# Graph network on one core: node scores spread over the partitions with two full-precision matmuls instead of four reduced-precision ones

## What is computed

```python
y = x @ w
s = y @ a
A = s[..., :, None] + s[..., None, :]
A = jnp.tanh(A / 8.0) * 8.0
A = jnp.where(A >= 0, A, 0.1 * A)
A = jnp.exp(A) * A_shape
A = A / jnp.sum(A, axis=-1, keepdims=True)
A = A * jnp.sum(A_shape, axis=-1, keepdims=True)
out = A @ x @ w
```

## Time and profile before

| | us |
|---|---|
| median of 3 runs | 1437.08 (1436.98 to 1437.58) |
| the profiled execution | 1435.79 |
| its span, first to last instruction | 1433.8 |
| PE busy | 1392.3 (97%) |
| DVE busy | 1287.9 (90%) |
| ACT busy | 990.5 (69%) |
| POOL busy | 947.7 (66%) |

### The profile page before, as it was taken

One profiled execution on the slowest core, in us unless ns is written; L12 is line 12 of the kernel. 1 busy time (PEld: TensorE's weight loads), 2 busy tenths in 40 slices (PEclk: granted clock), 3 DMA queues, 4 the chain that ended last, 5 costly groups with the idle time before them and its releaser, 6 DMA issues.

```text
span 1433.8 us, 34585 instructions
## 1 busy us (share of the span) xinstructions
PE 1392.3 (97%) x10900; PEld 1331.7 (93%) x10900; DVE 1287.9 (90%) x4001; ACT 990.5 (69%) x2312; POOL 947.7 (66%) x1876
## 2 busy tenths in 40 slices
PE   3799999999999999999999999999999999999997
PEld 2799999999999999999999999999999999999996
DVE  5789999999999999999999999999999999999984
ACT  3577777777777777777777777777777777777763
POOL 2676676676676676676676676676676676676652
PEclk9999999999999999999999999999999999999999
DMA  7011110120110110110110110110110110110100
GB/s 187 1 42 27 52 51 26 51 51 26 51 51 26 51 51 26 51 51 26 51 51 26 51 51 26 51 51 26 51 51 26 51 51 26 51 51 26 37 19 23
DMA packets 83078, 62.70 MB, mean 44 GB/s; under 512 B 40304, under 2 KB 65520, under 8 KB 83056
## 3 DMA queue, kind: packets, MB, share of 16 engines
q1 hardware_dynamic: 83056, 62.43, 15.8%
HBM read 45.62 MB, written 16.78 MB: 44 GB/s over the span
## 4 chain that ended last, share of the span: by engine, by line
PE 95%; DVE 2%; ACT 1%; issue 0%; DMA 0%; POOL 0%; SPq 0%; DVEq 0%; POOLq 0%
PE BANK L365 29%; PE BANK L330 24%; PE BANK L372 15%; PE WIDE L365 8%; PE WIDE L341 8%; PE WIDE L372 4%; PE BANK L357 2%; PE BANK L315 2%; PE BANK L384 2%; DMA TMP_D<-in_l2wt 0%; PE WIDE L278 0%; DVE BN_B L550 0%; DVE BN_C L550 0%; ACT UHI_D L444 0%; PE WIDE L284 0%
## 5 line engine op out<-in xcount | busy, mean ns | idle before, releaser
L444 ACT ACTIVATE UHI_B<-BANK 128x512 fp32r<-128x512 f32 x96 | 57.0, 593 | 43.9 <-PE BANK L330 43.9
L444 ACT ACTIVATE UHI_D<-BANK 128x512 fp32r<-128x512 f32 x96 | 57.1, 595 | 41.1 <-PE BANK L330 41.1
L444 ACT ACTIVATE UHI_C<-BANK 128x512 fp32r<-128x512 f32 x96 | 57.0, 594 | 41.0 <-PE BANK L330 41.0
L444 ACT ACTIVATE UHI_A<-BANK 128x512 fp32r<-128x512 f32 x96 | 57.1, 594 | 39.1 <-PE BANK L330 39.1
L599 DVE TENSOR_TENSOR ULO_D<-BANK,UHI_D 128x512 fp32r<-128x512 f32 x96 | 65.2, 680 | 18.7 <-ACT UHI_D L444 18.0
L732 POOL TENSOR_TENSOR LN_A<-MV_A,EPS 128x2 f32<-128x2 f32 x80 | 15.9, 198 | 92.3 <-DVE MV_A L558 92.3
L599 DVE TENSOR_TENSOR ULO_A<-BANK,UHI_A 128x512 fp32r<-128x512 f32 x96 | 65.2, 680 | 12.3 <-ACT UHI_A L444 11.8
L599 DVE TENSOR_TENSOR ULO_C<-BANK,UHI_C 128x512 fp32r<-128x512 f32 x96 | 65.1, 678 | 11.1 <-ACT UHI_C L444 9.3
L599 DVE TENSOR_TENSOR ULO_B<-BANK,UHI_B 128x512 fp32r<-128x512 f32 x96 | 65.7, 684 | 10.4 <-ACT UHI_B L444 8.5
L732 POOL TENSOR_TENSOR LN_D<-MV_D,EPS 128x2 f32<-128x2 f32 x80 | 15.8, 197 | 84.7 <-DVE MV_D L558 84.7
L732 POOL TENSOR_TENSOR LN_B<-MV_B,EPS 128x2 f32<-128x2 f32 x80 | 16.7, 209 | 78.2 <-DVE MV_B L558 78.2
(11 more groups left out here) (500 smaller groups left out, 6009.6 us busy)
## 6 DMA issues: line engine op xcount, KB each, us to landing
X_A<-in_xs SPq DMA_DIRECT2D x16, 256.0 KB, 2.8
X_B<-in_xs SPq DMA_DIRECT2D x16, 256.0 KB, 2.8
X_C<-in_xs SPq DMA_DIRECT2D x16, 256.0 KB, 2.8
X_D<-in_xs SPq DMA_DIRECT2D x16, 256.0 KB, 2.8
out_rows<-O_A SPq DMA_DIRECT2D x16, 256.0 KB, 2.0
out_rows<-O_B SPq DMA_DIRECT2D x16, 256.0 KB, 2.1
out_rows<-O_C SPq DMA_DIRECT2D x16, 256.0 KB, 2.1
out_rows<-O_D SPq DMA_DIRECT2D x16, 256.0 KB, 2.1
```

The source lines that it names most:

```text
L444: nc.scalar.activation(UHI[s][:, 0:J * D], bank(s, step)[:, :], ACT.Copy).then_inc(sem(f"c{step}"), 1)
```

## The change

The scores are no longer split. Steps 2H and 2L go from VectorE's list, and with them the tiles SHI and SLO and the reduced copy of the identity. TensorE's 3S waits for s_ready instead of scores_split, and does one matmul for each graph, on fp32 operands, instead of two on fp32r operands. All other steps keep their slots, and so their order.

```diff
-    "2U": 47.94, "2W": 50.48, "2S": 51.69, "2A": 52.99, "2N": 56.85, "2H": 56.91, "2L": 59.70, "3L": 66.92,
+    "2U": 47.94, "2W": 50.48, "2S": 51.69, "2A": 52.99, "2N": 56.85, "3L": 66.92,
...
-        IDENTR = sb("IDENTR", [P, P], F32R)
...
-        SHI = per_stream("SHI", J, dt=F32R)
-        SLO = per_stream("SLO", J, dt=F32R)
...
             def spread_scores(s, c, k):
 
-                pe.wait_ge(sem("scores_split"), c["n1"])
+                pe.wait_ge(sem("s_ready"), c["n1"])
                 bank_free(s, "3S", k)
                 for j in range(J):
-                    for part in (SHI, SLO):
-                        last = nc.tensor.matmul(bank(s, "3S")[:, j * P:(j + 1) * P], part[s][:, j:j + 1].to_broadcast([P, P]),
-                                                IDENTR[:, :], start=(part is SHI), stop=(part is SLO))
+                    last = nc.tensor.matmul(bank(s, "3S")[:, j * P:(j + 1) * P], ST[s][:, SC, j:j + 1].to_broadcast([P, P]),
+                                            IDENT[:, :], start=True, stop=True)
                 last.then_inc(sem("p3S"), 1)
...
                 dve.wait_ge(sem("ident_ready"), 1)
-                nc.vector.tensor_copy(IDENTR[:, :], IDENT[:, :])
...
-            def scores_high(s, c, k):
-                dve.wait_ge(sem("s_ready"), c["n1"])
-                nc.vector.tensor_copy(SHI[s][:, :], ST[s][:, SC, :]).then_inc(sem("s_high"), 1)
-
-            def scores_low(s, c, k):
-                dve.wait_ge(sem("s_high"), c["n1"])
-                nc.vector.tensor_tensor(SLO[s][:, :], ST[s][:, SC, :], SHI[s][:, :].bitcast(F32), ALU.subtract)\
-                    .then_inc(sem("scores_split"), 1)
```

More of the change, by code:

```diff
@@ L697, in _ @@
                      "1A": aggregate("1"), "2W": gcn_out, "2S": stats(RES, "2", "x2_ready"), "2A": aggregate("2"),
-                     "2N": node_scores, "2H": scores_high, "2L": scores_low, "3L": leak, "3E": attend, "3R": attention_sums,
+                     "2N": node_scores, "3L": leak, "3E": attend, "3R": attention_sums,
                      "3I": sums_inverse, "3J": sums_ratio, "3W": attention_out, "3S": stats(RES, "3", "c3W"),
```

## The result

The changed kernel takes 1438.63 us (1437.39 to 1440.85, 20 runs), and the kernel before, timed beside it, 1435.52 (1434.15 to 1437.62). The ratio is 1.0022, with a 95% interval from 1.0016 to 1.0029: 3.1 us slower. 1438.2 was forecast, from 1437.08 and a change of +1.1. The profiled execution took 1439.17, its span is 1437.1, 3.3 longer than before. The level of the kernel before moves by up to 4 us from one set of runs to the next (medians from 1435.52 to 1439.72), so the experiments are compared by ratio or within a set.

A forecast was written before the change was run, and what follows sets the result against it. TensorE was taken to bound the kernel (95% of the chain), with its short waits. -1.3 - 3.2 + 6.2 - 0.6 = +1.1 us, on the runs' median of 1437.08, gave 1438.2; range 1430 to 1446.

The forecast's parts named there:

- quarter A: Part of a pass from stream A's 3S start to the next 3S; 21.12 us, about 0.5 cheaper than the others.
- (1): TensorE's step 3S, two full-precision matmuls for four reduced ones: net -0.02 a step, times 64 = -1.3 us.
- The bound from incidences: Upper bound for 3S, from the only traced step of two full-precision matmuls, up to 0.57 us: +9.0 us.
- TensorE's rivals: The full-precision pair costs more on TensorE (0.12), 1448.5; or it takes twice the passes and 3S doubles (0.05), 1469.6.
- (2): VectorE's cast 2H, 0.73 us, goes; TensorE's product 1W hides it, so nothing is gained.
- (3): VectorE's rest 2L goes; last_bias, and leak where blocked, end 0.07 earlier: 45 x -0.07 = -3.2 us.
- the 45 quarters that were blocked: 15 passes of B, C and D, where VectorE's leak loses to GpSimd's last_bias; 1.48 us in C, 0.42 when free.
- (4): In quarter A last_bias would now start ahead of leak and block it: +0.41, times 15 = +6.2 us.
- the gap: Extra 0.10 us between VectorE's statistics and aggregate in quarter A (0.95, in C 0.85); moves if tied to an instruction-stream place.
- quarter C: Part of a pass from stream C's 3S, 21.65 us; last_bias starts 0.10 before leak, which takes 1.48.
- (5): First pass: TensorE waits 0.85 us for A's scores; VectorE loses cast and rest in the open: -0.6 us.

The follow-up runs named there:

- the version with the wait: Changed kernel with GpSimd's last_bias waiting for the next stream's leak: 1416.79 us; run again 1415.69, beside the kernel before with the same wait, 1416.58.
- the four versions with memsets: One-column setup memsets on VectorE: eleven in the kernel before (1445.36 us), five in it without 2L (1442.54), eleven (1441.19) and ten (1441.84) in the changed kernel.
- the memsets alone: Kernel before plus eleven one-column memsets in VectorE's setup, run once, loop untouched: 1445.36 us, ratio 1.0052.
- the rest alone: Kernel before without 2L, 3S multiplying the rounded scores twice: 1442.54 us with five setup memsets holding the aggregate's place, 1438.56 without them.
- TensorE's part alone: Kernel before with 3S in full precision after s_ready, VectorE still doing cast and rest, unused: 1434.7 us, ratio 0.9978.
- the small products: Two 128x2 products on GpSimd ahead of each last_bias: 1425.42 us in the kernel before, 1423.72 in the changed one.

## Why the prediction held, step by step

The number was met by 0.4 us, and part of that is luck. The forecast change was +1.1 us, and the measured one is +3.1. The sum began at 1437.08, and the kernel before, timed beside the changed one, took 1435.52. These two errors, 2.0 and 1.6, nearly cancel. What held is the mechanism: without the turn of quarter A, +6.2, the sum would have been -5.1, faster. The largest miss is the term of TensorE.

(1) *TensorE*: -0.02 a step was forecast. The 0.205 us a matmul came from a step of four full-precision matmuls that reduced ones would follow (0.81 in all). Where full-precision ones follow, such a step takes 0.89, or 0.222 a matmul; the kernel before has both side by side, 0U ahead of 4U (0.89) and 4U ahead of 3S (0.81). That I hadn't costed. The unit step before 3S now takes 0.89 in place of 0.81. 3S, with reduced ones behind it, takes 0.366, not 0.41. Together they take 1.259, before 1.290, so -0.03 where I had -0.06. The payment after it was as forecast, 0W 2.849 to 2.888, +0.04. Net +0.01 a step, +0.6 us in place of -1.3. The bound from incidences was no price: that step takes 0.36 in the version with the wait, so 0.2 of its 0.57 was a hidden wait, as suspected. TensorE's rivals fell with it.

(2) *The cast*: hidden, as said. VectorE waits 0.87 us for 1W now, in the timeline before L618.

(3) *The rest*: the statistics start 0.80 after conv_out, 0.86 before; last_bias leads leak by 0.17. But the 45 quarters that were blocked already gained 0.045 each in the mean, not 0.07 + 0.02. The cause is in 1W and 6W. These weight products have two forms: 1W 2.81 and 6W 1.36, or 2.91 and 1.41. Compared within a form the forecast of -0.09 was right: blocked quarters of the longer form went from 21.661 (17 steady ones) to 21.577 (47), of the shorter from 21.575 (25) to 21.480 (8). The mix moved to the longer form, and that took back about 2 us: 45 x 0.045 = 2.0. I had named it as what could make me wrong, without a price. Why a quarter takes one form isn't settled. All steady quarters with a free leak have the longer one, and so have all those of the four versions with memsets.

(4) *Quarter A's race*: +0.41 x 15 = +6.2 was forecast, and 21.554 - 21.143 = 0.411 is what it came to. The mechanism holds in its parts: the memsets alone flip A, the rest alone flips A in 14 of 15 passes, the gap follows instruction 460. The margin was misread, because it has two values. In the steady quarters last_bias starts 2.54 to 2.56 after the aggregate and 0.65 after L756, whether leak runs or not, so the 0.07 by which it stood behind leak in the earlier trace rows was a real lag. But it belongs to the passes in which the 1W and 6W ahead had the shorter form, nine of the 15; in the others the two started level, within 0.02 us, but for the first (0.25). The 0.10 in quarter C of the earlier trace rows is of the longer form. So the 0.17 between the two quarters that I compared was 0.10 of gap and 0.07 of form, and last_bias now leads by 0.17 in A's passes of the longer form (13 of 15) where I had 0.10. With the rest alone gone all of A's passes had the longer form, and level became a lead of 0.07. With the shorter form it would have been about nothing, as forecast, which no run shows. The change moves A's aggregate by ten places, not eleven; instruction 460 lies behind leak either way.

By the Trainium skill, "Runtime: NRT & Kernel Launch", section "Instruction fetch mechanics", crossing from one block of instructions to the next is mostly hidden. The runs agree with a place in the stream, and with "mostly": only where the aggregate stands at it is anything seen. Through a race those 0.10 us weighed 0.41 us a pass in the change and 0.54 with the memsets, 6 to 8 us in all. That it is a fetch was not shown.

(5) *First pass*: 3S of A waits 0.27 us, not 0.85; -0.6 was forecast. From TensorE's timeline, the changed kernel and then TensorE's part alone:

```profile
60.95 0.68 PE L380 MATMUL BANK<-IDENT,ST_A 128*128 128x128 f32 x4 [0.27 <-DVE RES_B L618]
```

```profile
60.86 0.68 PE L383 MATMUL BANK<-IDENT,ST_A 128*128 128x128 f32 x4 [0.85 <-DVE RES_B L621]
```

What is waited for is no longer the scores but conv_out of stream B. Waiting for s_ready alone gained nothing, 0.85 again, and the version with only the rest gone waits 0.84. So it is the cast that had to go: in the first pass it isn't hidden, which the prediction had as well. In its start one program differs between two executions by more (61.69 and 59.86 for the same kernel with the wait), so only the wait's row bears this out, not the 0.65 between 61.60 and 60.95.

In sum: (1) +0.6, (3) without it -2.5, (4) without it +6.0, (5) -0.6 give +3.5; the spans differ by 3.3.

## What to carry to other kernels

When two engines block each other, look at the start times on both sides for a near tie, and ask who wins in each part of the loop; a change that moves either by 0.1 us, or that only adds or removes instructions ahead, can turn it, and the price is the length of the blocked operation, not of what was edited. Where the order matters, say it with a semaphore: here one wait on an engine with time to spare was worth over 20 us, seven times what the change under study moved. And judge an edit with the race settled the same way in both kernels, or the race is what is measured.

## What the runs showed of the hardware

VectorE and GpSimd shut each other out for whole instructions: leak took 0.42 us ahead of last_bias and 1.40 to 1.56 behind it, and a two-column operation 0.16 or 1.30. The Trainium skill, "SBUF — State Buffer", section "SBUF: two separate sides", calls the pair's shared port an exclusive lock that goes to whoever starts first; the rows agree, down to leads of 0.02 us.

The aggregate starts 0.10 us late in each pass of the loop where it is instruction 460 of VectorE's program, 0.35 in the first, and only there. Where another instruction stands there, it starts no later in the loop's first pass than in the others. Eleven memsets that run once in the setup made the kernel 7 us slower (1445.36 against 1437.95), most of it through the race.

Two full-precision matmuls of 128 columns take 0.365 us, four reduced ones 0.478, when reduced ones follow. But the neighbours take it back: a full-precision step takes 0.08 more when full-precision matmuls follow it (0.89 against 0.81 for four), and the reduced step behind them 0.04 more than behind reduced ones (0W 2.888 against 2.849).

With the small products in place of the wait, most weight products of TensorE run longer (1W 2.933 against 2.914, 3W 1.505 against 1.467, 2W 1.508 against 1.472; 0W does not, 2.880 against 2.888), and the steps together make the whole of 21.32 against 21.18. No run tells why.
